# Attention and experts on one core: output products behind the value products, scores re-dealt over the units, the fourth gather ahead of a low half

## The chip, the cores and the metric

The kernel runs on one core of one Trainium2 chip. The metric is the device time of one execution in microseconds. Before the change: median 290.72 us of 3 runs (289.91 to 291.37).

## What is computed

The input x has 4 x 512 tokens of 512 channels. Per token it is normalized; then an attention with 8 heads of 8 channels over each batch of 512 tokens, and an expert layer with two experts of eight per token, are both applied to the normalized rows and added to x:

```python
xn  = layernorm(x)
qk  = (xn @ Wqk.T + bqk)  -> q, k of 8 heads, 8 channels each;   v = xn @ Wv.T + bv
att = softmax(q @ k.T, axis=-1) / sqrt(64)
a   = (att @ v) @ Wo.T + bo
y_e = relu(xn @ We[e] + be[e]);   top 2 of (xn @ Wgate + bgate)
out = x + a + mean over the two chosen experts of y_e
```

Everything is to be exact to fp32 closely, so products are made of a high and a low part of their operands.

## The kernel before

**Projection and routing** (lines 1235 to 1394). The 16 row tiles are normalized (ScalarE, row_mid), written to DRAM as xn_rows, transposed on TensorE and projected to q, k, v and gate logits. DVE then finds the two experts of each token; TensorE counts tokens per expert (counts, lines 1365 to 1375), DVE works out the place of each token in a list of 39 tiles of 128 rows, sorted by expert (lines 986 to 1022), and sets gather_i (the rows to gather) and expert_i (the expert of each tile; semaphore experts_known). The list is known a little before the gathers can deliver, and TensorE fills the time with matmuls that nothing reads ("unread").

**Expert tiles** (lines 1402 to 1430). For each of the 39 tiles POOL gathers 128 rows of xn_rows into one of six row_in buffers (gather, line 608; the first six at lines 615 to 620, with the low half of a weight chunk, low_half(7), ahead of the fourth). TensorE transposes tile n + 1 (turn_rows) and then multiplies tile n: 12 matmuls of 512 columns (line 1421), three for each of four channel blocks: t_hi by high weights, t_hi by low weights, t_lo by high weights. ScalarE makes t_hi from the transposed rows (774), DVE makes t_lo (1039). Behind tile n DVE adds the bias (1082), ScalarE does relu (779), POOL adds half of the output bias (637), SP stores the tile. The weights of experts 4 to 7 are split while the first tiles run: ScalarE the high part, DVE the low part (late_low, one chunk of 1024 columns at a time, line 1031), two before the loop, one in iteration 0 and one in each of iterations 1 to 5. DVE's iteration n is: t_lo of tile n, bias add of tile n - 1, then a late low half, then the maxima of tile n - 1.

**Scores and their ring.** Softmax needs each row's maximum ahead of the logits. So TensorE computes scores (queries by keys of one head, 32 rows of contraction, 512 columns, line 1283) into PSUM banks of a ring, DVE takes the maximum of each (line 1051), and the negated maxima are put into q_t as two more channels. Batches 0 and 1 have their scores behind the expert tiles: four behind each second tile from tile 5 on. In the tiles the ring has four banks. Batches 2 and 3 (64 scores) have theirs in the attention phase, where the ring has three banks.

**Attention units** (lines 1432 to 1451). A unit (b, u) is one batch, four heads and one block of 128 keys: 32 units. TensorE does for each: the first logit pair (two heads, line 1310), the unit's first half of scores, its jobs, the second logit pair, its second half of scores, and the value products of the unit before (line 1341, four heads side by side). ScalarE takes the exponential of each pair (line 818, 1024 columns). A pair waits until ScalarE has read the same pair's bank of the unit before; values wait for both exponentials of their unit.

Jobs (unit_jobs, line 257) are the further work that shares the ring: "k" and "q" (transposes of laid-out keys and queries, kept by ScalarE), "max" (transposes of the row maxima, kept by ScalarE), "o" (transposes of the value sums of the batch before; DVE divides them and splits them in lay_both, line 1104), "turn" (transposes back, waits for lay_both through o_laid, kept by ScalarE) and "out" (the output product, two matmuls at lines 1271 and 1272; DVE adds it to acc in result, line 1133, and SP stores it). In batches 1 to 3 unit 2 has "o", unit 3 "turn", units 4 to 7 "out" (in batch 3: two in unit 4, one in 5, one in 6). The list ring (lines 311 to 317) holds scores and jobs in TensorE's order; item n uses bank n mod 3 and waits until the item before it on that bank has been read. DVE serves its items in the same order: maxima of the first half, jobs, maxima of the second half. spread_scores (line 294) deals the 64 scores evenly over 48 half units from (0, 1) to (3, 0): one or two each, 2.67 per unit.

**Other queues.** POOL adds the experts' rows to acc by 32 indirect transfers during the attention. SP's queue, in order of code: loads of acc, move_max (eight small transfers that bring the maxima into q_t; the one for (2, 1) stands behind the first four stores), stores.

## Time and profile before

| | |
|---|---|
| median of 3 runs | 290.72 us (289.91 to 291.37) |
| profiled execution: its own time | 289.8 us |
| its span | 288.0 us |
| TensorE (PE) busy | 273.8 us (95%) |
| VectorE (DVE) busy | 211.6 us (73%) |
| ScalarE (ACT) busy | 162.1 us (56%) |
| GpSimd (POOL) busy | 193.3 us (67%) |
| projection and routing | 0 to about 58 us |
| expert tiles | about 60 to 198 us |
| attention units, with the last sums and stores | about 198 to 288 us |

"Busy" is the time in which an engine has an instruction under way. Matmuls are pipelined, so one of 512 columns is shown as 0.4 to 0.5 us while the next starts 0.23 us later: for TensorE, differences between starts say more than durations. "[0.69 <-DVE row_max L1051]" at the end of a timeline row means that the engine was idle 0.69 us before it and that this instruction of DVE released it.

### The profile page before, as it was taken

The page shows a single profiled execution, that of the slowest core. Times are in us where ns is not written, and L with a number is a line of the kernel's source. Part 1 is how long each engine was busy: PE and PEld are TensorE (multiplying, and loading weights), DVE is VectorE, ACT ScalarE, POOL GpSimd, SP SyncE. Part 2 cuts the span into 40 slices and gives each one's busy share as a digit, 9 for nine tenths or more (in the row PEclk, how much of TensorE's full clock was granted, in tenths as well). Part 3 has the DMA queues.
Part 4 walks back from the last instruction along what each step waited for, and adds up shares of the span by engine and source line. Part 5 has one row for each costly group of instructions (what it writes and reads, how often), then busy time and mean ns, then how long its engine had stood idle before and what let it go on. Part 6 is the DMA issues. An engine that isn't in the chain of part 4 may idle for free.

```text
span 288.0 us, 5481 instructions
## 1 busy us (share of the span) xinstructions
PE 273.8 (95%) x1685; PEld 180.2 (63%) x1685; DVE 211.6 (73%) x433; ACT 162.1 (56%) x241; POOL 193.3 (67%) x221
## 2 busy tenths in 40 slices
PE   6999998979999999999999999999999999999994
PEld 2699995567877777788777778774332333333342
DVE  2998898987877787767777776675678888784233
ACT  2669999256333333344333334436999878779861
POOL 3278997599866766898586866425788877887100
PEclk9799999799999999999999999999999999999999
DMA  7999899766544454435444445312599999999713
GB/s 213 388 400 397 287 278 404 268 225 201 178 164 148 146 146 149 147 110 184 148 149 147 150 146 150 110 73 75 190 221 262 262 253 236 198 209 183 158 67 146
DMA packets 28086, 57.35 MB, mean 199 GB/s; under 512 B 3287, under 2 KB 3608, under 8 KB 27804
## 3 DMA queue, kind: packets, MB, share of 16 engines
q1 hardware_dynamic: 19792, 37.59, 36.5%
q0 software_dynamic: 7728, 18.62, 30.0%
q10 hardware_dynamic: 540, 0.80, 0.8%
q8 instruction: 15, 0.25, 0.4%
q14 instruction: 11, 0.09, 0.1%
HBM read 38.29 MB, written 18.61 MB: 198 GB/s over the span
## 4 chain that ended last, share of the span: by engine, by line
PE 77%; DVE 8%; DMA 5%; issue 2%; POOL 2%; ACT 2%; SPq 1%; ACTq 0%; POOLq 0%
PE ps_l L1421 36%; PE ps_o L1341 7%; PE ps_l L1310 6%; PE ps_l L1399 6%; PE ps_l L1231 6%; PE ps_r L1283 3%; PE ps_l L1215 2%; PE ps_r L1259 2%; DMA w_split<-in_L_attn_Wv_w_dram 2%; DMA row_in<-xn_rows,gather_i 2%; DMA q_t<-max_rows 2%; PE ps_r L1271 2%; DVE row_max L1051 2%; ACT probs L818 1%; POOL row_in L612 1%
## 5 line engine op out<-in xcount | busy, mean ns | idle before, releaser
L1421 PE MATMUL ps_l<-w_split,t_hi 128*128 x312 | 100.1, 402 | 0.3 <-issue 0.3
L1051 DVE TENSOR_REDUCE row_max<-ps_r 128x1 f32<-128x512 f32 x112 | 73.0, 682 | 10.1 <-PE ps_r L1283 9.9
L637 POOL TENSOR_TENSOR row_mid<-row_mid,bias_o 128x512 f32<-128x512 f32 x39 | 51.4, 1319 | 35.5 <-ACT row_mid L779 35.4
L779 ACT ACTIVATE row_mid<-row_mid 128x512 f32<-128x512 f32 x39 | 24.7, 633 | 84.0 <-DVE row_mid L1082 84.0
L818 ACT ACTIVATE probs<-ps_l 128x1024 f32<-128x1024 f32 (+1 forms) x63 | 62.0, 1012 | 11.7 <-PE ps_l L1310 11.2
L1421 PEld LDWEIGHTS ps_l<-w_split,t_hi 128*128 128x128 f32 x312 | 55.8, 189 | 10.7 <-issue 0.8
L1421 PE MATMUL ps_l<-w_split,t_lo 128*128 x156 | 61.3, 393 | 0.0
L674 POOL DMA_INDIRECT acc<-expert_rows,slots_i x32 | 49.6, 1551 | 12.9 <-issue 7.2
L1082 DVE TENSOR_TENSOR row_mid<-ps_l,bias_e 128x512 f32<-128x512 f32 x39 | 27.0, 691 | 32.8 <-PE ps_l L1421 32.7
L612 POOL DMA_INDIRECT row_in<-xn_rows,gather_i x39 | 40.8, 1046 | 9.1 <-issue 2.9
L1421 PEld LDWEIGHTS ps_l<-w_split,t_lo 128*128 128x128 f32 x156 | 29.3, 188 | 6.6
L1283 PE MATMUL ps_r<-k_t,q_t 32*128 32x512 f32 x112 | 32.5, 489 | 0.2
L1310 PEld LDWEIGHTS ps_l<-q_t,k_t 32*128 32x128 f32 x124 | 11.3, 181 | 32.7 <-ACT probs L818 18.6
L1310 PE MATMUL ps_l<-q_t,k_t 32*128 32x512 f32 x124 | 29.7, 492 | 0.8 <-DMA q_t<-max_rows 0.4
L1039 DVE TENSOR_TENSOR t_lo<-ps_l,t_hi 128x512 fp32r<-128x512 f32 x39 | 26.9, 690 | 4.7 <-ACT t_hi L774 4.0
L1399 PE MATMUL ps_l<-ident,row_in 128*128 128x128 f32 x156 | 24.4, 279 | 1.6 <-DMA row_in<-xn_rows,gather_i 1.6
L774 ACT ACTIVATE t_hi<-ps_l 128x512 fp32r<-128x512 f32 x39 | 22.7, 582 | 3.8 <-PE ps_l L1399 3.8
L1399 PEld LDWEIGHTS ps_l<-ident,row_in 128*128 128x128 f32 x156 | 17.7, 141 | 8.8 <-issue 5.1
L1231 PE MATMUL ps_l<-wp_hi,t_hi 128*128 128x208 f32 x64 | 18.9, 295 | 1.0 <-DVE t_lo L919 0.4
L570 POOL TENSOR_TENSOR w_split<-w_split 128x1024 fp32r<-128x1024 f32 x8 | 19.0, 2395 | 0.6 <-ACT w_split L712 0.6
L1231 PE MATMUL ps_l<-wp_lo,t_hi 128*128 128x208 f32 x64 | 17.8, 278 | 0.0
L1231 PE MATMUL ps_l<-wp_hi,t_lo 128*128 128x208 f32 x64 | 17.7, 277 | 0.0
(218 smaller groups left out, 402.0 us busy)
## 6 DMA issues: line engine op xcount, KB each, us to landing
expert_rows<-row_mid SPq DMA_DIRECT2D x39, 256.0 KB, 2.0
xn_rows<-row_mid SPq DMA_DIRECT2D x16, 256.0 KB, 5.2
w_split<-in_L_ffn_W_e_dram SPq DMA_DIRECT2D x8, 512.0 KB, 5.6
w_split<-in_L_ffn_W_e_dram SPq DMA_DIRECT2D x4, 1024.0 KB, 11.0
acc<-in_L_attn_x_dram SPq DMA_DIRECT2D x16, 256.0 KB, 10.0
out_dram<-res SPq DMA_DIRECT2D x16, 256.0 KB, 3.7
row_in<-in_L_attn_x_dram SPq DMA_DIRECT2D x8, 256.0 KB, 5.9
w_split<-in_L_attn_x_dram SPq DMA_DIRECT2D x8, 256.0 KB, 7.1
```

The lines of the kernel that those rows point to most:

```text
L612: pool.indirect_dma_start(row_in[:, n % RI, :], None, xn_dram, bass.IndirectOffsetOnAxis(ap=gather_i[:, n:n + 1], axis=0)).then_inc(rows_i ...
L637: pool.tensor_tensor(row_mid[:, n % 4, :], row_mid[:, n % 4, :], bias_o[:], ALU.add).then_inc(y_done, 1)
L674: pool.indirect_dma_start(acc[:, i, :], None, y_dram, bass.IndirectOffsetOnAxis(ap=slots_i[:, r, i:i + 1], axis=0), compute_op=ALU.add).th ...
L818: act.activation(probs[:, n % 2, 2 * half:2 * half + 2, cs], logit_pair(half)[:, :, cs], ACT.Exp).then_inc(exp_done, 1)
L1039: dve.tensor_tensor(t_lo[:, n % 2, :], ps_t[:, n % 2, :], t_hi[:, n % 2, :].bitcast(F32), ALU.subtract).then_inc(rows_lo, 1)
L1051: dve.tensor_reduce(row_max[:, b % 2, h, i:i + 1], ring_bank(item), AX.X, ALU.max).then_inc(freed_by_dve, 1)
L1082: dve.tensor_tensor(row_mid[:, (n - 1) % 4, :], ps_y[:, (n - 1) % 2, :], bias_e[:, bass.ds(e, 1), :].rearrange("p a h -> p (a h)"), ALU.ad ...
L1231: mm = pe.matmul(ps_y[:, i % 2, 0:PW], a[:, i % 2, ks], w[:, c, :], start=(n == 0), stop=(n == 3 * KC - 1))
L1283: pe.matmul(ring_bank(item), q_t[b][rows, g, i * P:(i + 1) * P], k_t[b][rows, g, :], start=True, stop=True).then_inc(scores_ready, 1)
L1310: mm = pe.matmul(logit_pair(half)[:, k, :], k_t[b][rows, g, kt * P:(kt + 1) * P], q_t[b][rows, g, :], start=True, stop=True)
L1399: mm = pe.transpose(ps_t[:, n % 2, c * P:(c + 1) * P], row_in[:, n % RI, c * P:(c + 1) * P], ident[:])
L1421: mm = pe.matmul(ps_y[:, n % 2, :], a[:, n % 2, ks], rhs, start=(k == 0), stop=(k == 3 * KC - 1))
```

## The change

- In units whose jobs are all "o" or "out" (jobs_behind, but not (3, 6)), TensorE runs the jobs behind the value products, DVE serves them behind the maxima of the second half, and the ring lists them there. These are (1, 2), (1, 4) to (1, 7), (2, 2), (2, 4), (2, 6), (2, 7), (3, 4) and (3, 5). Units with a "turn", and (2, 5), which has a "max" too, keep their order.
- Scores are dealt by shares: units with an "o" or an "out" have 2, the others 3. It comes to two in ten units, three in twelve, four in (1, 3) and (3, 0).
- The four scores of tile 5 are put ahead of the first tile, between three and six unread matmuls that take the place of ten.
- POOL issues the fourth gather ahead of the low half.
- DVE's late low halves: none in iteration 0, one in each of iterations 1 to 6. They get a semaphore of their own, late_lo_made.
- The count of each expert gets P/2 - 0.5 from one more matmul (a new bf16 tile, rounding, with its semaphore; their declarations are left out below), and DVE takes the larger of that and P/2 + 0.5 where it added P/2 - 0.5, so an expert without tokens gets a tile too.

```diff
--- before.py
+++ after.py
@@ -53,6 +53,7 @@
 FIRST_UNIT_AT = NS - 2
 assert SCORES_AT[0] + H * QT // 2 <= SCORES_AT[1] and SCORES_AT[1] + H * QT // 2 <= FIRST_UNIT_AT
 FIRST_HALF, HALVES = 2, 48
+LIGHT, FULL = 2, 3
 BY_ROWS = [(b, g) for b in range(B - 1) for g in range(G)]
 
 
@@ -265,6 +269,10 @@
                     6: [("out", b - 1, 2)], 7: [("out", b - 1, 3)]}.get(u, [])
             return plan + (last if b >= 1 else [])
 
+        def jobs_behind(b, u):
+
+            return bool(unit_jobs(b, u)) and all(job[0] in ("o", "out") for job in unit_jobs(b, u)) and (b, u) != (B - 1, 2 * HG - 2)
+
         def tile_jobs(n):
 
             return {14: [("max", 0, 0)], 18: [("k", 1, 0), ("k", 1, 1)],
@@ -295,9 +303,17 @@
 
             halves = [[] for t in range(2 * 2 * HG * B)]
             left = [("score", b, g * HG + j, i) for b in range(2, B) for g in range(G) for i in range(QT) for j in range(HG)]
+            shares = [0]
+            for k in range(HALVES // 2):
+                b, u = divmod(FIRST_HALF // 2 + k, 2 * HG)
+                shares.append(shares[-1] + (LIGHT if any(job[0] in ("o", "out") for job in unit_jobs(b, u)) else FULL))
+
+            def due(k, part):
+                return (2 * H * QT * shares[k] + part * shares[-1]) // (2 * shares[-1])
+
             for k in range(HALVES):
                 t = FIRST_HALF + k
-                for n in range(2 * H * QT * k // HALVES, 2 * H * QT * (k + 1) // HALVES):
+                for n in range(due(k // 2, k % 2), due(k // 2 + 1, k % 2)):
                     taken = [item[2] % HG for item in halves[t]] + [2 * (t % 2), 2 * (t % 2) + 1]
                     item = [item for item in left if item[2] % HG not in taken][0]
                     left.remove(item)
@@ -314,7 +330,10 @@
         for b in range(B):
             for u in range(2 * HG):
                 t = 2 * (2 * HG * b + u)
-                ring += half_scores[t] + unit_jobs(b, u) + half_scores[t + 1]
+                if jobs_behind(b, u):
+                    ring += half_scores[t] + half_scores[t + 1] + unit_jobs(b, u)
+                else:
+                    ring += half_scores[t] + unit_jobs(b, u) + half_scores[t + 1]
         in_tiles = 4 + sum(len(tile_scores(n) + tile_jobs(n)) for n in range(NS))
         last_jobs = [job for u in range(HG, 2 * HG) for job in unit_jobs(B - 1, u)]
         in_bank = {item: n % (RING + 1) if n < in_tiles else (n - in_tiles) % RING for n, item in enumerate(ring)}
@@ -531,6 +550,7 @@
             pool.affine_select(out=ident[:], in_=ident[:], compare_op=ALU.not_equal, fill=1.0, base=0,
                                pattern=[[-1, P]], channel_multiplier=1).then_inc(consts_ready, 1)
             pool.memset(eps_t[:], EPS).then_inc(consts_ready, 1)
+            pool.memset(rounding[:], (P / 2 - 0.5) / P).then_inc(rounding_set, 1)
             link(pool.memset(ones[:], 1.0))
             pool.affine_select(out=before[:], in_=ones[:], compare_op=ALU.is_gt, fill=0.0, base=0,
                                pattern=[[1, P]], channel_multiplier=-1).then_inc(consts_ready, 1)
@@ -615,8 +635,9 @@
             for n in range(RI):
                 if n == 3:
 
+                    pool.wait_ge(experts_known, 1)
+                if n == 4:
                     low_half(NW - 1)
-                    pool.wait_ge(experts_known, 1)
                 gather(n)
 
             pool.wait_ge(half_bias, 1)
@@ -849,7 +870,7 @@
                     for half in range(2):
                         if 2 * n + half > 2:
                             exponentials(n, half)
-                        if half == 0:
+                        if half == jobs_behind(b, u):
                             for job in unit_jobs(b, u):
                                 if job[0] in KEPT:
                                     keep(*job)
@@ -983,7 +1004,7 @@
             dve.wait_ge(counted, 1)
             ps_c = ps_y[:, 0, 0:(NT + 1) * NE].rearrange("p (i e) -> p i e", e=NE)
 
-            link(dve.tensor_scalar(ecol[:, 1, :], ps_c[:, NT, :], P / 2 - 0.5, BY_128, ALU.add, ALU.add))
+            link(dve.tensor_scalar(ecol[:, 1, :], ps_c[:, NT, :], P / 2 + 0.5, BY_128, ALU.max, ALU.add))
 
             dve.wait_ge(ramp_ready, 4)
             link(dve.scalar_tensor_tensor(out=tri[:], in0=ecol[:, 1:2, :].to_broadcast([P, NE, NE]), scalar=-BY_128, in1=lower_ps,
@@ -1029,7 +1050,7 @@
                 dve.wait_ge(w_hi_made, c + 1)
                 cs = slice(2 * half, 2 * half + 2)
                 dve.tensor_tensor(w_split[:, e, 1, cs, :], w_split[:, e, 1, cs, :].bitcast(F32), w_split[:, e, 0, cs, :].bitcast(F32),
-                                  ALU.subtract).then_inc(w_lo_made, 1)
+                                  ALU.subtract).then_inc(late_lo_made, 1)
 
             dve.wait_ge(wo_split, 1)
             dve.tensor_tensor(by_columns(wo_lo), wo_ps, by_columns(wo_hi).bitcast(F32), ALU.subtract).then_inc(wo_split, 1)
@@ -1068,8 +1089,6 @@
             for n in range(NS + 1):
                 if n < NS:
                     rows_low(n)
-                if n == 0:
-                    late_low(NW + 2)
                 if n >= 1:
                     e = dve.value_load(expert_i[0:1, n - 1:n], min_val=0, max_val=NE - 1)
                     dve.wait_ge(y_made, n)
@@ -1083,8 +1102,8 @@
                                       ALU.add).then_inc(y_biased, 1)
                     if n == NS - 1:
                         lay_max(1, 1)
-                    if NW + 2 + n < 2 * NE:
-                        late_low(NW + 2 + n)
+                    if NW + 1 + n < 2 * NE:
+                        late_low(NW + 1 + n)
                     for item in tile_maxima(n - 1):
                         maximum(item)
                         if item == group_scores[item[1], item[2] // HG][-1] and n < NS - 2:
@@ -1157,7 +1176,7 @@
                             maximum(item)
                             if item == group_scores[item[1], item[2] // HG][-1]:
                                 lay_max(item[1], item[2] // HG)
-                        if half == 0:
+                        if half == jobs_behind(b, u):
                             serve(unit_jobs(b, u))
 
             def lay_half(piece):
@@ -1368,6 +1387,8 @@
             for i in range(last):
                 behind = NT - i
                 pe.matmul(counts[:, i + 1:NT + 1, :], ones[:], mask[:, i:i + 1, :].to_broadcast([P, behind, NE]), start=False, stop=False)
+            pe.wait_ge(rounding_set, 1)
+            pe.matmul(counts[:, NT, :], ones[:], rounding[:], start=False, stop=False)
             unread(2)
             pe.wait_ge(mask_ready, 3)
             pe.matmul(counts[:, last, :], before[:], mask_last[:, 0, :], start=False, stop=False)
@@ -1387,7 +1408,7 @@
             mm.then_inc(tokens_found, 1)
             for job in ring[2:4]:
                 fill(*job)
-            unread(10, D, ps_y[:, 0, :])
+            unread(3, D, ps_y[:, 0, :])
 
             def turn_rows(n):
                 pe.wait_ge(rows_in[n % RI], 16 * (n // RI + 1))
@@ -1399,6 +1420,9 @@
                     mm = pe.transpose(ps_t[:, n % 2, c * P:(c + 1) * P], row_in[:, n % RI, c * P:(c + 1) * P], ident[:])
                 mm.then_inc(rows_turned, 1)
 
+            for item in tile_scores(SCORES_AT[0]):
+                scores(item)
+            unread(6, D, ps_y[:, 0, :])
             pe.wait_ge(experts_known, 1)
             turn_rows(0)
             for n in range(NS):
@@ -1412,7 +1436,10 @@
                     pe.wait_ge(y_biased, n - 1)
                 if n < NE:
                     pe.wait_ge(w_hi_made, 2 * (n + 1))
-                    pe.wait_ge(w_lo_made, 2 * (n + 1))
+                    if n < LATE:
+                        pe.wait_ge(w_lo_made, 2 * (n + 1))
+                    else:
+                        pe.wait_ge(late_lo_made, 2 * (n + 1 - LATE))
                 k = 0
                 for c in range(KC):
                     ks = slice(c * P, (c + 1) * P)
@@ -1421,7 +1448,7 @@
                         mm = pe.matmul(ps_y[:, n % 2, :], a[:, n % 2, ks], rhs, start=(k == 0), stop=(k == 3 * KC - 1))
                         k += 1
                 mm.then_inc(y_made, 1)
-                for item in tile_scores(n):
+                for item in tile_scores(n) if n != SCORES_AT[0] else ():
                     scores(item)
                 for job in tile_jobs(n):
                     if job[0] == "first":
@@ -1441,7 +1468,7 @@
                         values(0, 0)
                     if n == LAST:
                         logits(b, u, 1)
-                    for job in unit_jobs(b, u):
+                    for job in unit_jobs(b, u) if not jobs_behind(b, u) else ():
                         fill(*job)
                     if n < LAST:
                         logits(b, u, 1)
@@ -1449,6 +1476,8 @@
                         scores(item)
                     if n >= 2:
                         values(*divmod(n - 1, 2 * HG))
+                    for job in unit_jobs(b, u) if jobs_behind(b, u) else ():
+                        fill(*job)
             values(B - 1, 2 * HG - 1)
             for kind, part in TAIL:
                 if kind == "o":
```

## Rows read from the trace of the kernel before

**Rows 1.** Waits of PE from 57 us on; us in total, times, longest us.

```profile
PE ps_l L1399 <- DMA row_in<-xn_rows,gather_i: 1.6, 3, 0.7
PE ps_r L1267 <- DVE row_max L1051: 1.1, 2, 0.7
PE ps_r L1249 <- DVE row_max L1051: 0.6, 1, 0.6
```

**Rows 2.** Busy time by stretch of units: us, PE, PEld, DVE, ACT, POOL, PEclk, DMA, GB/s.

```profile
200.10:218.16 18.06, 17.35 (x128) 6.30 (x124) 13.38 (x23) 17.03 (x23) 13.89 (x16) 1.00 0.80 209
219.98:225.61 5.63, 4.94 (x41) 1.84 (x37) 5.33 (x12) 4.92 (x6) 4.78 (x6) 1.00 1.11 263
225.61:236.31 10.70, 10.70 (x71) 3.75 (x67) 9.36 (x17) 8.40 (x9) 8.59 (x6) 1.00 1.11 256
236.31:246.65 10.34, 9.35 (x72) 3.19 (x68) 8.73 (x18) 8.76 (x11) 8.07 (x6) 1.00 1.12 232
246.65:258.13 11.48, 11.36 (x71) 4.15 (x72) 9.19 (x15) 8.66 (x9) 9.54 (x7) 1.00 1.04 202
258.13:262.23 4.10, 3.78 (x33) 1.14 (x29) 2.59 (x6) 3.56 (x5) 3.49 (x3) 1.00 1.06 217
```

**Rows 3.** Timeline, 59 to 67 us: POOL and PE; start us, us, engine line.

```profile
59.22 2.38 POOL L570 TENSOR_TENSOR w_split<-w_split 128x1024 fp32r<-128x1024 f32 x1
...
61.77 1.77 POOL L612 DMA_INDIRECT row_in<-xn_rows,gather_i  x1 [0.16 <-issue]
...
66.88 0.65 PE L1399 MATMUL ps_l<-ident,row_in 128*128 128x128 f32 x4 [0.29 <-DMA row_in<-xn_rows,gather_i]
```

**Rows 4.** Busy time of one microsecond before the tiles; PEclk is the third from the end.

```profile
52.00:53.00 1.00, 0.93 (x14) 0.58 (x15) 0.88 (x3) 0.00 (x0) 0.00 (x0) 0.51 1.08 438
```

**Rows 5.** Timeline of PE: first matmuls of tiles 5, 6 and 7.

```profile
76.89 0.71 PE L1421 MATMUL ps_l<-w_split,t_hi 128*128 x2
...
80.68 0.70 PE L1421 MATMUL ps_l<-w_split,t_hi 128*128 x2
...
83.88 0.71 PE L1421 MATMUL ps_l<-w_split,t_hi 128*128 x2
```

**Rows 6.** Timeline of DVE: last late low half, bias add of tile 5.

```profile
77.45 1.21 DVE L1031 TENSOR_TENSOR w_split<-w_split 128x1024 fp32r<-128x1024 f32 x1
...
80.05 0.69 DVE L1082 TENSOR_TENSOR row_mid<-ps_l,bias_e 128x512 f32<-128x512 f32 x1 [0.64 <-PE ps_l L1421]
```

**Rows 7.** Timeline of DVE: four maxima back to back, behind lay_both.

```profile
222.87 2.59 DVE L1051 TENSOR_REDUCE row_max<-ps_r 128x1 f32<-128x512 f32 x4
```

**Rows 8.** Timeline of PE in unit (1, 5): product, second pair, values; next unit.

```profile
228.78 0.50 PE L1271 MATMUL ps_r<-wo_hi,o_t 128*128 128x512 f32 x1
...
229.44 0.50 PE L1310 MATMUL ps_l<-q_t,k_t 32*128 32x512 f32 x2
...
229.87 1.05 PE L1341 MATMUL ps_o<-probs,v_second 128*18 128x512 f32 x8
230.85 0.50 PE L1310 MATMUL ps_l<-q_t,k_t 32*128 32x512 f32 x2
```

**Rows 9.** Timeline of PE in the last unit: both logit pairs, values.

```profile
276.10 0.70 PE L1310 MATMUL ps_l<-q_t,k_t 32*128 32x512 f32 x4
276.73 0.62 PE L1341 MATMUL ps_o<-probs,proj 128*9 128x256 f32 x8
```

**Rows 10.** Timeline of ACT: exponentials back to back, and of unit (1, 5).

```profile
218.79 3.77 ACT L818 ACTIVATE probs<-ps_l 128x1024 f32<-128x1024 f32 x4
...
228.88 2.12 ACT L818 ACTIVATE probs<-ps_l 128x1024 f32<-128x1024 f32 x2 [0.61 <-PE ps_l L1310]
```

**Rows 11.** Timeline: transposes of the sums, start of lay_both, the turn.

```profile
220.42 0.66 PE L1263 MATMUL ps_r<-ident,o_sum 128*128 128x128 f32 x4
...
221.17 0.35 DVE L1098 RECIPROCAL o_inv<-ps_r 128x32 f32<-128x32 f32 x1
...
223.61 0.66 PE L1267 MATMUL ps_r<-ident,o_tok 128*128 128x128 f32 x4 [0.69 <-DVE row_max L1051]
```

3 lines of the change are left out of this document (added).

## Prediction

> **What bounds the kernel now.** The page first: TensorE is busy for nearly all of the span and the other engines are not. But a full TensorE row does not mean that its order is free: where a matmul waits for a bank inside a group, the profile draws a longer busy stretch. So the waits come next, then the timeline round each place that the change touches. After the routing three waits stand out: 1.6 us for gathered rows, 1.1 us before the "turn" transposes and 0.6 us before the "max" ones, the last two for DVE's row maxima [rows 1]. Then I cut the attention phase at the first logit pairs of units [rows 2], since a unit's period is what this change is paid in: (1,4) to (1,7), each with one output product, take 10.70 us, 2.68 each.
>
> **Before the tiles.** POOL starts the low half (2.38 us) at 59.22 and issues gather 3 only at 61.77; its rows reach TensorE at 66.88, after 0.29 us of idleness [rows 3]. With gather 3 ahead, it goes out near 59.4, its rows land before 65 and tile 2 starts 0.3 earlier. The low half then ends near 63.4 and gather 4 goes out about when it does now; experts_known, now waited for first, is set long before. The low half is for tile 3, some seven microseconds later. **0.3 gained** (0 to 0.5).
>
> Three unreads, four scores and six unreads take the place of ten unreads. The four scores lie in four row groups, so they run together. The cover is TensorE's wait for the first gather, the longest of the three, 0.7 [rows 1]; without it the scores would cost 0.6. I take nothing (bound: 0.3 lost). TensorE's clock was at 1.2 GHz (0.51) in this stretch, where it had idled and then run small matmuls [rows 4].
>
> What the scores should bring in tile 5: that tile takes 3.79 us start to start with them, the next 3.20 without [rows 5], so 0.59. But the last late low half moves into DVE's iteration 6, where two maxima stand. From the tile's end DVE then does the bias add (0.6 to its next start), the low half (1.21) [rows 6] and two maxima (0.64 each) [rows 7] before t_lo of tile 7 (0.69): 80.05 + 0.61 + 1.22 + 1.28 + 0.69 = 83.85, where TensorE would want it at 83.88 - 0.59 = 83.29 [rows 5]. It waits 0.6, and the gain is gone. **Net 0** (0.6 gained to 0.2 lost). The other late low halves come a tile later into iterations without maxima. The rounding matmul runs while TensorE waits for mask_last, POOL's memset lies in its early slack, add and max are one DVE instruction either way, and two semaphores in place of one change no time of arrival: nothing. With the cover gone each would cost under 0.3.
>
> **Products behind the values.** Such a unit now runs: first pair and score (0.43 to the next start, like the second), product (0.66), second pair (0.43), values (0.98), 2.50 in all [rows 8]. Its three sisters share the other 8.20, 2.73 each; they have three scores: a score waits for the ring's bank. Behind the values, the two pairs touch each other. The last unit's two pairs take 0.63 without scores [rows 9]; with two scores I take 0.70. Period 0.70 + 0.98 + 0.67 = 2.35. ScalarE allows it: an exponential starts 0.54 after its pair (228.88; the pair 0.44 before the product of 228.78), and four back to back take 3.77, 0.94 each [rows 10], so the next unit's second pair may start some 0.54 + 0.94 + 0.94 + 0.14 for the last one's end = 2.56 after this unit's first. From there pair, values and product are 2.08 more: 4.64 for two units, 2.32 each. So 10.70 becomes 9.40: **1.3 gained** (0.3 to 2.0). The Trainium skill (TensorEngine Tiling (Array Packing), Key Properties) says that a change of tiling mode drains TensorE; three changes in place of four would by that save one drain, and the trace agrees: a lone pair 0.43, two together 0.63.
>
> (2,4) to (2,7) take 11.48 [rows 2]. Three go to 2.35. In (2,5), which keeps its order, the second pair's score waits now for the bank of ("max",3,0), freed by ScalarE behind an exponential; the new ring puts it on a bank that DVE frees sooner, and I take 2.9. Sum 9.95: **1.5 gained** (0.4 to 2.0). (3,4) and (3,5), three products in two units, by the same differences: **0.35 gained** (0 to 0.6).
>
> **Sums behind the values.** Here the move costs. The transposes of the sums start at 220.42, 0.44 into unit (1,2); lay_both begins 0.75 after and lasts 1.70 to DVE's next instruction; one maximum later the turn's bank is free, 223.61, 3.63 into a stretch of 5.63 [rows 2, 7, 11]. After: the second pair waits for ScalarE until 0.80, values at 1.23, sums at 2.2, lay_both 2.96 to 4.7, turn at 4.8, since it now waits for lay_both itself. Then the second pair (5.39), and DVE's maxima of (1,3)'s two first scores, queued behind lay_both: (1,3) has four scores, and the fourth uses the bank of the second, free at 6.04. Values 6.46, next unit 7.44. **1.8 lost** (0.6 to 2.1). In (2,2) and (2,3) the turn's unit has three scores, so that last wait is absent: about 6.85. Before them (2,0) gets a third score on the bank of its first; DVE has the result of ("out",0,3) and that maximum to do, so it goes at 1.45 and the unit takes 2.9, and (2,1) some 1.85. Together 11.6 against 10.34 [rows 2]: **1.2 lost** (0 to 1.6). SP issues store(3) ahead of move_max(2,1); its result comes later but before the maximum is kept, so the moves wait for nothing new.
>
> **More scores in the full units.** Of 24 units 14 now have three or four, 10 have two. (0,1), (0,4) and (0,7) gain one. ("max",1,1) in (0,2) waits 0.6 for DVE already [rows 1]; with one maximum more ahead of it (0.64), unit (0,3) starts 0.65 later. The other two lose 0.3 each, as their second score waits for a bank. ScalarE hides little of it: it is busy 17.03 of 18.06 there [rows 2]. **1.25 lost** (0 to 1.9). (3,0) gets a fourth score on its own first one's bank, behind a result: (3,0) and (3,1) take 4.55, now 4.10 [rows 2]: **0.45 lost** (0 to 1.0).
>
> **Sum.** -0.3 + 0 - 1.3 - 1.5 - 0.35 + 1.8 + 1.2 + 1.25 + 0.45 = +1.25. The profiled execution took 289.8 us (span 288.0), 0.9 under the median, so by it the changed kernel would take 291.0, and by the median 290.72 + 1.2 = **291.9**. A measurement of this kernel tells some 0.5%, 1.45 us, from no change; this is inside.
>
> **Rivals.** *The losses are absorbed* (faster). Each loss is a wait for a bank or for lay_both that I put on the path in full. If ScalarE's queue, nearly full before (1,2), sets the period there, the added scores and (2,0) lose nothing (1.25 + 0.45 + 0.8, the 0.8 for (2,0), = 2.5 less), and tile 5 may keep half of its 0.6. For: 17.03 of 18.06. Against: the 0.6 before "max" shows TensorE on the path. 1.25 - 2.5 - 0.3 = -1.55: 289.2.
>
> *The ring of three binds in the full units* (slower). A unit with three scores and a job takes four turns of three banks. If each of the ten or so such units up to (2,3) loses 0.17 beyond my terms, the sum is +2.95: 293.7. It decides once DVE no longer idles ahead of a unit's first maximum; it is busy 5.33 of 5.63 in the stretch from 219.98 [rows 2]. The Trainium skill (the same page, PSUM Bottleneck) warns that after fourfold tiling the copies out of PSUM may bind; the trace agrees for that stretch alone.
>
> *The clock falls in the turn's longer stall* (slower). TensorE would stand for some 1.5 us in (1,3). Should the clock go to 1.2 GHz as before the tiles [rows 4], four microseconds at half rate cost up to 2: 293.9. Against: with today's stall it stayed at 1.00 [rows 2]. The Trainium skill (TensorE: Matmul & The Clock Gate, What's actually happening) calls the throttled state the default that activity releases.
>
> That the change does not do what it says can hold for the scores in the gap alone, and is in the sum.
>
> **How the numbers follow.** Forecast 0.47, its own range 290.4 to 293.2; it lies close to the bound, so 0.35 of it counts as no change and 0.12 as slower. Absorbed 0.32 (0.25 faster, 0.07 no change). Ring 0.16, clock 0.05. Faster 0.25, same 0.42, slower 0.33. The range takes in the absorbed case and nearly the ring's, and so most of the bounds of the terms, which hardly fall all on one side: 288.9 to 293.6.
>
> **What would show it.** Right: turn 00 about 4.8 us behind the start of (1,2), with DVE's lay_both named; (1,4) to (1,7) in 9.4; tile 2 0.3 earlier; a new wait of 0.6 before tile 7; (2,0) near 2.9. Wrong: product units still at 2.5, or at 2.1; the turn at 3.6; (0,2) to (1,2) no longer than now; a granted clock below 1 after the tiles have begun.

## The result, and the profile after

The changed kernel took 294.64 us (median of 4 runs, 294.16 to 296.58) against 290.32 for the kernel before in the same comparison: ratio 1.0164, 95% interval 1.0101 to 1.0228. It is slower, by over three times the 1.25 us forecast, and above the range (288.9 to 293.6). The profiled execution took 294.16 us, span 292.4; before 289.8 and 288.0. Ratios here leave out executions that took over 1.5% more than the fastest of their kernel, so they can lie below the ratio of the medians.

The four largest waits of TensorE from 57 us on: engine, line and releaser; us in total, times, longest.

```profile
PE ps_r L1286 <- DVE o_tok L1133: 4.6, 2, 3.0
PE ps_l L1420 <- DMA row_in<-xn_rows,gather_i: 2.1, 2, 1.3
PE ps_l L1448 <- issue: 0.8, 2, 0.6
PE ps_r L1302 <- DVE row_max L1072: 0.8, 2, 0.6
```

L1286 is the turn (L1267 before), and its two waits have gone from 1.1 us for a row maximum [rows 1] to 4.6 for `o_tok`, the last operation of lay_both. That wait was forecast, though not 3.0 us of it in one piece.

The attention phase, cut at first logit pairs as in [rows 2]: (0,1) to (1,1), (1,2) and (1,3), (1,4) to (1,7), (2,0) and (2,1), (2,2) and (2,3), (2,4) to (2,7), (3,0) and (3,1), (3,2) to (3,6). Columns: us, PE, PEld, DVE, ACT, POOL, granted clock, DMA, GB/s.

```profile
197.78:221.00 23.22, 22.00 (x154) 7.64 (x153) 17.72 (x30) 19.83 (x26) 18.23 (x19) 1.00 0.81 206
221.00:228.42 7.42, 5.45 (x42) 2.01 (x38) 6.19 (x15) 5.12 (x6) 5.73 (x7) 1.00 1.10 261
228.42:237.69 9.27, 9.27 (x68) 3.14 (x64) 7.35 (x12) 7.58 (x8) 7.67 (x5) 1.00 1.12 237
237.69:242.45 4.76, 4.24 (x33) 1.25 (x32) 3.81 (x7) 4.03 (x7) 4.01 (x3) 1.00 1.11 278
242.45:252.32 9.87, 6.55 (x41) 2.30 (x38) 6.36 (x14) 5.23 (x6) 8.35 (x6) 0.83 1.02 171
252.32:262.26 9.94, 9.94 (x72) 3.55 (x68) 7.04 (x11) 8.20 (x9) 8.11 (x7) 1.00 1.04 192
262.26:267.08 4.82, 4.12 (x30) 1.21 (x29) 3.45 (x7) 3.82 (x6) 2.78 (x2) 1.00 1.05 229
267.08:280.52 13.44, 13.29 (x105) 5.67 (x101) 5.18 (x13) 11.73 (x14) 0.00 (x0) 1.00 0.34 90
```

Cut at the same places, the kernel before has 21.30, 5.64, 10.69, 4.18, 6.16, 11.48, 4.10 and 13.87 us. So the phase has grown by 5.32, and one stretch holds most of that: (2,2) and (2,3), 6.16 to 9.87, the only one with a clock below 1.00. (Unit (0,1) begins 0.9 earlier than before, and 0.8 of that is there already when the first tile's rows are transposed, at 57.34 against 58.14. It is not the change: the profiles below, which all have its first part, start there anywhere from 57.32 to 58.25. The span grows by 4.4.)

What happens in (1,3), TensorE first and then DVE:

```profile
223.21 0.66 PE L1282 MATMUL ps_r<-ident,o_sum 128*128 128x128 f32 x4
...
225.85 0.63 PE L1286 MATMUL ps_r<-ident,o_tok 128*128 128x128 f32 x4 [1.55 <-DVE o_tok L1133]
```

```profile
223.91 0.36 DVE L1117 RECIPROCAL o_inv<-ps_r 128x32 f32<-128x32 f32 x1 [0.84 <-PE ps_r L1282]
...
225.28 0.43 DVE L1133 TENSOR_TENSOR o_tok<-o_exact,o_tok 128x256 f32<-128x256 f32 x1
225.62 2.06 DVE L1072 TENSOR_REDUCE row_max<-ps_r 128x1 f32<-128x512 f32 x3
```

Sums at 2.2 into (1,2), lay_both from 2.9 to 4.6, turn at 4.85, three maxima queued behind. That is the forecast's sequence to 0.1 us. In (2,3) the same sequence looks like this:

```profile
244.72 0.66 PE L1282 MATMUL ps_r<-ident,o_sum 128*128 128x128 f32 x4
...
248.83 1.09 PE L1286 MATMUL ps_r<-ident,o_tok 128*128 128x128 f32 x4 [3.02 <-DVE o_tok L1133]
249.85 0.79 PE L1329 MATMUL ps_l<-q_t,k_t 32*128 32x512 f32 x2
...
250.58 1.81 PE L1360 MATMUL ps_o<-probs,proj 128*9 128x512 f32 x8
252.32 0.49 PE L1329 MATMUL ps_l<-q_t,k_t 32*128 32x512 f32 x2
```

```profile
246.60 0.36 DVE L1117 RECIPROCAL o_inv<-ps_r 128x32 f32<-128x32 f32 x1 [1.37 <-PE ps_r L1282]
```

And the single microseconds around it:

```profile
247.00:248.00 1.00, 0.00 (x0) 0.00 (x0) 0.93 (x3) 0.67 (x1) 0.90 (x1) 1.00 1.12 180
248.00:249.00 1.00, 0.17 (x1) 0.20 (x2) 0.96 (x3) 0.00 (x0) 0.69 (x2) 0.88 0.92 133
249.00:250.00 1.00, 1.00 (x7) 0.67 (x6) 0.89 (x2) 0.04 (x1) 1.00 (x1) 0.50 0.94 152
...
252.00:253.00 1.00, 1.00 (x13) 0.32 (x11) 0.10 (x1) 0.14 (x1) 0.69 (x2) 0.91 0.95 135
```

Read it in two parts. First, lay_both starts 1.88 us after the sums' transposes instead of 0.70, and the turn stands 6.4 into the pair of units instead of 4.85: 1.5 us that are lost before the clock column falls. Second, TensorE idles through 247 and most of 248, then comes back at 1.2 GHz until 252. Turn, pair and values take 1.02, 0.73 and 1.74 us start to start there, against 0.56, 0.43 and 0.97 in units at full clock: another 1.5 us. Together these are the 3.0 us by which the stretch misses its forecast of 6.85. (The whole fall lasts 3.4 us, from 248.76 to 252.17: it begins at the very end of the wait.)

A product unit (one with an "out" job) after the change, (1,5), values and product turned round against [rows 8]:

```profile
230.73 0.49 PE L1329 MATMUL ps_l<-q_t,k_t 32*128 32x512 f32 x2
...
231.42 1.05 PE L1360 MATMUL ps_o<-probs,v_second 128*18 128x512 f32 x8
232.41 0.50 PE L1290 MATMUL ps_r<-wo_hi,o_t 128*128 128x512 f32 x1
...
233.07 0.49 PE L1329 MATMUL ps_l<-q_t,k_t 32*128 32x512 f32 x2
```

Both pairs 0.69, values 0.99, product 0.66: 2.34, where 0.70, 0.98 and 0.67 were forecast.

In the expert tiles, POOL near 59 us, DVE and then TensorE near 81 us:

```profile
58.71 0.95 POOL L632 DMA_INDIRECT row_in<-xn_rows,gather_i  x1 [0.30 <-issue]
59.68 2.43 POOL L590 TENSOR_TENSOR w_split<-w_split 128x1024 fp32r<-128x1024 f32 x1
```

```profile
79.35 1.49 DVE L1052 TENSOR_TENSOR w_split<-w_split 128x1024 fp32r<-128x1024 f32 x1
80.76 1.28 DVE L1072 TENSOR_REDUCE row_max<-ps_r 128x1 f32<-128x512 f32 x2
81.96 0.68 DVE L1060 TENSOR_TENSOR t_lo<-ps_l,t_hi 128x512 fp32r<-128x512 f32 x1
```

```profile
81.65 0.60 PE L1420 MATMUL ps_l<-ident,row_in 128*128 128x128 f32 x4
82.84 0.72 PE L1448 MATMUL ps_l<-w_split,t_hi 128*128 x2 [0.59 <-issue]
```

Gather 3 now stands ahead of the low half, and tile 2 waits for no rows. The wait moved to tile 7 is there: DVE's low half, two maxima and t_lo are late by 0.6.

### The profile page after: what moved, and what is told of

Read it like the earlier page. It is cut to its first block, busy times and chain, and to the rows that moved or that the text cites. A ratio compares the mean times of both kernels' runs of the same rounds, so it can differ in the third digit from the quotient of the medians.

```text
span 292.4 us, 5482 instructions
## 1 busy us (share of the span) xinstructions
PE 272.5 (93%) x1685; PEld 179.3 (61%) x1685; DVE 211.6 (72%) x433; ACT 161.9 (55%) x241; POOL 195.9 (67%) x222
## 4 chain that ended last, share of the span: by engine, by line
PE 77%; DVE 14%; issue 3%; DMA 2%; ACT 2%; POOL 1%; SPq 0%; DVEq 0%; POOLq 0%; ACTq 0%
PE ps_l L1448 37%; PE ps_o L1360 9%; PE ps_l L1420 7%; PE ps_l L1329 5%; PE ps_l L1250 5%; PE ps_r L1302 3%; DVE row_max L1072 2%; PE ps_r L1278 2%; PE ps_r L1290 2%; DVE t_lo L940 1%; PE ps_l L1234 1%; DMA row_in<-in_L_attn_x_dram 1%; DMA row_in<-xn_rows,gather_i 1%; ACT probs L839 1%; PE ps_r L1282 1%
## 5 line engine op out<-in xcount | busy, mean ns | idle before, releaser
L658 POOL TENSOR_TENSOR row_mid<-row_mid,bias_o 128x512 f32<-128x512 f32 x39 | 50.6, 1297 | 32.9 <-ACT row_mid L800 32.3
L839 ACT ACTIVATE probs<-ps_l 128x1024 f32<-128x1024 f32 (+1 forms) x63 | 61.2, 1012 | 13.2 <-PE ps_l L1329 11.5
L632 POOL DMA_INDIRECT row_in<-xn_rows,gather_i x39 | 44.1, 1130 | 9.1 <-issue 3.6
L1302 PE MATMUL ps_r<-k_t,q_t 32*128 32x512 f32 x112 | 31.8, 486 | 1.3 <-DVE row_max L1072 0.8
L1329 PE MATMUL ps_l<-q_t,k_t 32*128 32x512 f32 x124 | 26.8, 488 | 0.6 <-issue 0.3
L1302 PEld LDWEIGHTS ps_r<-k_t,q_t 32*128 32x128 f32 x112 | 12.6, 182 | 8.8 <-issue 5.0
```

The lines of the kernel that those rows point to most:

```text
L632: pool.indirect_dma_start(row_in[:, n % RI, :], None, xn_dram, bass.IndirectOffsetOnAxis(ap=gather_i[:, n:n + 1], axis=0)).then_inc(rows_i ...
L658: pool.tensor_tensor(row_mid[:, n % 4, :], row_mid[:, n % 4, :], bias_o[:], ALU.add).then_inc(y_done, 1)
L839: act.activation(probs[:, n % 2, 2 * half:2 * half + 2, cs], logit_pair(half)[:, :, cs], ACT.Exp).then_inc(exp_done, 1)
L1302: pe.matmul(ring_bank(item), q_t[b][rows, g, i * P:(i + 1) * P], k_t[b][rows, g, :], start=True, stop=True).then_inc(scores_ready, 1)
L1329: mm = pe.matmul(logit_pair(half)[:, k, :], k_t[b][rows, g, kt * P:(kt + 1) * P], q_t[b][rows, g, :], start=True, stop=True)
```

## The experiments

The main theory: the sums behind the values make the turn wait for lay_both, the dealing of scores lengthens the full units, and on top the longer idleness lets TensorE's clock fall. The rivals: the clock is chance of an execution or chip and the price is that of the order alone; or one of the two parts carries all of it. The kernel before took 289.81 us (median of 22 runs), 290.02 (29) and 290.3 (23) in the three comparisons below. All experiments start from the changed kernel; e1 to e12 are the names that the quoted expectations use.

**e1.** **The changed kernel once more**, no edit.

> The changed kernel once more, to see which of its stalls come back. Theory (the turns wait for lay_both, and the longer of the two stalls lets the clock fall): the ratio is 1.012 to 1.020, the turn of (2,3) waits over 2 us again and TensorE's clock is at 0.5 in some four microseconds behind it. Rival (the 3.0 us stall and the clock fall are an accident of that one execution, and the kernel's steady loss is 1.8 in (1,3) plus the added scores): the turn of (2,3) waits some 1.6 us as that of (1,3) does, the clock stays at 1.00, and the span is some 3 us shorter than 292.4.

294.43 us (8 runs, 291.0 to 298.95), ratio 1.0094 (1.0055 to 1.0133). Every run comes with its mean granted clock, and among these eight the time goes with it: 291.0 at 0.988 and 291.15 at 0.994, but 298.77 at 0.951 and 298.95 at 0.954. Between kernels or series the mean is a poor guide, since it counts falls ahead of the tiles too: in the first four executions of this same program 0.988 goes with 294.16 and 294.76. The profile is of the 298.77 one. Its rows: (0,1) to (1,1), (1,2) and (1,3), (1,4) to (1,7), (2,2) and (2,3).

```profile
198.13:223.83 25.70, 24.25 (x155) 8.18 (x154) 18.00 (x30) 20.17 (x26) 19.41 (x20) 0.87 0.83 211
223.83:232.48 8.65, 6.39 (x43) 2.02 (x40) 6.73 (x15) 5.12 (x6) 7.36 (x7) 0.88 1.11 257
232.48:243.79 11.31, 11.31 (x69) 3.67 (x65) 7.00 (x11) 7.59 (x8) 9.48 (x7) 0.79 1.09 211
248.54:256.38 7.84, 6.00 (x41) 1.90 (x37) 5.78 (x14) 5.17 (x6) 6.62 (x5) 0.86 1.01 158
```

Three falls in one execution: 203 to 210, 230 to 237 and 254 to 258 us. Against the first profile of the same program the first costs 2.5 us (25.70 against 23.22), the second 3.3 (19.96 against 16.69, of which 0.3 is a longer wait). The turns waited 1.82 and 1.54 here, so the 3.0 of the first profile does not come each time, as the rival had it. The clock fell behind the turn of (2,3) again, as the theory had it. Falls come and go between executions of one program.

**e2.** **Sums and turn back in their old order**, products still behind the values, dealing as changed.

```diff
-return bool(unit_jobs(b, u)) and all(job[0] in ("o", "out") for job in unit_jobs(b, u)) and (b, u) != (B - 1, 2 * HG - 2)
+return bool(unit_jobs(b, u)) and all(job[0] == "out" for job in unit_jobs(b, u))
```

> The changed kernel with the sums of (1,2) and (2,2) back between the logit pairs; products stay behind the values, scores are dealt as in the change. Theory: nearly all of the loss is the two turns waiting for lay_both, so it takes 5 us less than the changed kernel, 289.5 to 290, a ratio of 0.995 to 1.000; (1,2) and (1,3) together take 5.6 to 6.2 in place of 7.4, (2,2) and (2,3) 6.0 to 6.4 in place of 9.9. Rival (DVE, late because of the four scores of (1,3) and the added scores before it, sets the turn whichever side the sums are on): the two pairs of units still take over 7 and 8, and the ratio stays above 1.010.

289.79 us (10 runs), ratio 1.002 (0.9991 to 1.0049). Rows as for the last kernel.

```profile
198.31:223.69 25.38, 24.18 (x154) 8.18 (x153) 17.73 (x30) 20.15 (x26) 19.81 (x21) 0.87 0.83 209
223.69:229.98 6.29, 5.41 (x43) 2.01 (x39) 6.06 (x15) 5.13 (x6) 5.52 (x6) 1.00 1.10 262
229.98:239.21 9.23, 9.23 (x70) 3.14 (x66) 7.35 (x12) 7.60 (x8) 7.49 (x6) 1.00 1.12 241
243.96:250.04 6.08, 5.18 (x43) 2.02 (x39) 5.71 (x14) 4.91 (x6) 5.17 (x4) 1.00 1.11 209
```

Moving the sums alone is worth the 4.6 us between this median and that of e1 (0.7% by the ratios). The two places where the order differs give 7.42 - 6.29 = 1.1 and 6.88 (from e5, below) - 6.08 = 0.8 of it at full clock. The other 2.7 us are not read off a stretch; what the profiles show beside the order is the falls behind the turns. The clock fell once here too, from 203 to 210, in (0,2) to (0,4), where the scores are dealt as changed. (The edit drops the exception of (3,6) as well, so its product stands behind its values here, in e6, e7, e11 and e12; the unit takes 2.96 against 2.94.)

**e3.** **The scores dealt evenly, as before; order as changed.**

```diff
-                for n in range(due(k // 2, k % 2), due(k // 2 + 1, k % 2)):
+                for n in range(2 * H * QT * k // HALVES, 2 * H * QT * (k + 1) // HALVES):
```

> The changed kernel with the scores dealt evenly over the 48 half units as before; sums and products stay behind the values. Theory (the dealing loses 1.9 before (1,2), 0.7 in (3,0) and 0.6 in (2,0), and gives back under 1 in the product units): some 2 us less than the changed kernel, a ratio of 1.005 to 1.010, with the turns' waits still there. Rival (the order alone makes the loss and the light units are what makes the product units fast): no less than the changed kernel, 1.015 or more, with product units at 2.5.

293.13 us (4 runs), ratio 1.0134 (1.0102 to 1.0165). The median is 1.3 us below that of e1, but the ratio is not lower, so the gain of 2 us that the theory had is not clear. (0,1) to (1,1) is back at 21.32, so the dealing made the +1.9 there. But (1,4) to (1,7) takes 10.62, nothing gained: (1,5), with two scores, takes 2.31, and of the three with three scores (1,4) takes 2.33 but (1,6) and (1,7) take 2.99 and 3.00, more than the 2.73 of three scores in the old order. The clock falls at 248 to 251, behind the turn of (2,3).

**e4.** **Both back; what is left is the change's first part** (gather, scores in the gap, late halves).

```diff
-return bool(unit_jobs(b, u)) and all(job[0] in ("o", "out") for job in unit_jobs(b, u)) and (b, u) != (B - 1, 2 * HG - 2)
+return False
...
-                for n in range(due(k // 2, k % 2), due(k // 2 + 1, k % 2)):
+                for n in range(2 * H * QT * k // HALVES, 2 * H * QT * (k + 1) // HALVES):
```

> Only what the change does ahead of the attention units: fourth gather first, scores in the gap, late low halves a tile later, the rounding matmul; order of jobs and dealing of scores are those of before. Theory: 0 to 0.4 us less than before, a ratio of 0.998 to 1.001; tile 2 starts without the wait for gathered rows and tile 7 waits some 0.6 for t_lo. Rival (the 0.59 of tile 5 is kept): a ratio of 0.996 to 0.997.

289.76 us (10 runs), ratio 0.9989 (0.9959 to 1.0019), as the theory had it. Its units take what they took before, within 0.05 in every stretch, and the clock does not fall from 57 to 285 us. So all of the loss is in the units, and the first part is worth nothing that can be measured.

**e5.** **The changed kernel with TensorE kept at work in the turns' stall.** Six matmuls of which nothing reads the result, behind the wait for the bank they write; the result of the kernel is the same.

```diff
+HELD = {(1, 3): 6, (2, 3): 6}
...
+                    if (b, u) in HELD:
+                        pe.wait_ge(exp_done, 2 * n - 2)
+                        unread(HELD[b, u], D, ps_y[:, 0, :])
```

> The changed kernel with six matmuls that nothing reads (512 columns, into the bank of the second logit pair, once its exponential is done) ahead of the turns of (1,3) and (2,3), inside the wait for lay_both. The waits for lay_both stay and TensorE is not idle in them. Theory (the changed kernel pays 1.8 and some 1.7 us for the waits themselves and, in most executions, 2 to 4 us more because TensorE's clock falls in or behind them): the clock is 1.00 from 225 to 285 in the profile, (1,3) still takes about 4.6 and (2,3) 4 to 5, the median is 291 to 292.5, a ratio of 1.005 to 1.009, and executions scatter less. A fall near 203, ahead of the first held turn, can still come. Rival (the clock falls for another reason than the idle turn, or costs nothing): the median stays at 294 and the clock still falls behind (1,3) or (2,3). Should the six cost more than the wait hides, (1,3) takes over 5.

TensorE and the microsecond behind the turn of (2,3):

```profile
245.48 1.47 PE L1377 MATMUL ps_l<-ones 128*128 128x512 bf16 x6
247.09 0.63 PE L1287 MATMUL ps_r<-ident,o_tok 128*128 128x128 f32 x4
247.65 0.50 PE L1330 MATMUL ps_l<-q_t,k_t 32*128 32x512 f32 x2
```

```profile
248.00:249.00 1.00, 1.00 (x11) 0.12 (x8) 0.83 (x2) 1.00 (x2) 0.69 (x2) 1.00 0.90 145
```

The filler delays the turn by nothing (it stands 4.91 into the pair of units, as in e1), and the clock stays: (2,2) and (2,3) take 6.88, against 9.87 and 7.84 in the two profiles of the changed kernel. But the median is 293.48 us (6 runs, 291.6 to 294.59), ratio 1.0125 (1.0089 to 1.0161): in its profile the clock fell at 263 to 266 instead, in (3,1), and (3,0) to (3,6) took 19.83 against 18.26. No wait of TensorE over 0.4 us stands in the ten microseconds ahead of that fall. So work in the gap of (2,3) went with a held clock there, in one profile, and holding two places doesn't hold the clock of the kernel. The expectation of a gain in the median was not met.

This profile also gives the price of order and dealing at full clock. Its units from (0,1) to (3,6) take 81.12 us; without the 1.6 of that fall (19.83 - 18.26) it is 79.5, against 77.4 in the kernel before: 2.1 us.

**e6.** **Products behind their values, scores dealt evenly, sums in their old place** (both edits shown above, that of the sums and that of the dealing).

> Products behind the values, scores dealt evenly as before, sums between the pairs, the edits ahead of the units as in the change: against e4_before_units it is the order of the products alone. Theory (with a third score the product unit waits for a bank in either order, 2.73 against 2.99; with two it takes 2.31 in place of 2.51, and (3,4) and (3,5) give 0.45): -0.1 to -0.6 us against e4, a ratio of 0.996 to 1.000. Rival (the order alone gives the 2.31 of the changed kernel in every product unit): 2.5 us less than e4, a ratio of 0.990.

289.09 us (12 runs), ratio 0.9978 (0.9951 to 1.0005), as the theory had it.

**e7.** **Scores dealt by hand**: two in a product unit, but never more than three in another, and none of the sums moved.

```diff
-FIRST_HALF, HALVES = 2, 48
-LIGHT, FULL = 2, 3
+FIRST_HALF, HALVES = 2, 50
+DEAL = ((1, 1), (2, 1), (1, 2), (2, 1), (2, 1), (1, 2), (1, 1),
...
-                for n in range(due(k // 2, k % 2), due(k // 2 + 1, k % 2)):
+                for n in range(DEAL[t // 2 - 1][t % 2]):
```

> The version that the readings point to: products behind the values, sums between the pairs, scores dealt over 50 half units: two in (0,1), (0,7), (2,0) and all units with a product, three in the others up to (3,1), so that no unit has four and (0,2) waits as before. Theory: the product units keep 2.31 (1.4 and 1.5 us gained), (3,4) and (3,5) 0.45; lost are some 0.5 in (0,4), 0.3 in (1,2), 0.2 in (2,3), 0.1 in (3,1). Sum -2.3: 287.5, a ratio of 0.990 to 0.994, and the clock stays at 1.00 from 60 to 285. Rival (the ring binds in the full units wherever the scores are put, so what is gained in the product units comes back there): a ratio of 0.998 to 1.003, with (2,0) to (2,4) and (3,0) to (3,2) longer than 10.34 and 4.10 by what the product units gain.

288.61 us (12 runs), ratio 0.9958 (0.9934 to 0.9982): 0.4% faster than the kernel before. It is short of the 287.5 expected; (3,2), which was not in the sum, takes 3.86 in place of 2.86.

**e8.** **The same dealing, with the products in the old order too** (the last edit, and jobs behind no unit's values).

> The dealing of e7 with all jobs between the logit pairs, as before the change: against e7 it is the order of the products with two scores each, against e4 the dealing alone. Theory: product units at 2.51 in place of 2.31, so 1.4 + 0.45 us more than e7, 289.4, and 0 to 0.7 less than e4. Rival (the fewer scores alone make the 2.31, since they take the bank waits away): the same time as e7.

289.48 us (12 runs), ratio 0.9995 (0.997 to 1.0021). The stretch (1,4) to (1,7) of the last three kernels in their order, even dealing with products behind, by hand with products behind, by hand with products between:

```profile
224.94:235.57 10.63, 10.36 (x71) 3.53 (x67) 9.04 (x16) 7.96 (x9) 8.25 (x6) 1.00 1.11 255
```

```profile
225.62:234.86 9.24, 9.24 (x69) 3.22 (x65) 7.30 (x13) 7.80 (x9) 7.71 (x6) 1.00 1.11 251
```

```profile
225.53:235.55 10.02, 10.02 (x68) 3.21 (x64) 8.21 (x14) 8.25 (x9) 8.01 (x6) 1.00 1.11 257
```

With the 10.69 of old order and even dealing (e4) all four combinations of two orders and two dealings are there. Order alone gives 0.06, dealing alone 0.67, both 1.45: under the even dealing (1,4), (1,6) and (1,7) have a third score, and in (1,6) and (1,7) it goes only 0.9 us into the unit (in (1,7) the trace names DVE's result, which frees its bank) and eats what the order saves. In (1,4) DVE had been idle for 0.72 us at its first maximum, and the third score costs nothing there.

**e9.** **Only the sums of (1,2) and (2,2) behind their values**, all else as in the kernel with both back.

```diff
+            return (b, u) in ((1, 2), (2, 2))
```

> Scores dealt evenly and products between the pairs, as before the change; only the sums of (1,2) and (2,2) stand behind their values (with the edits ahead of the units, as in e4_before_units). It is the price of that one move. Theory: the turns wait for lay_both, (1,2) and (1,3) take 6.8 and (2,2) and (2,3) 7.0 to 7.3 in place of 5.7 and 6.2, so 2 us more than e4 where the clock stays up and 3 to 4 where it falls: a median of 291.8 to 293.5, a ratio of 1.006 to 1.013, with the clock at 0.5 behind a turn in some executions. Rival (alone the move costs little, and it takes DVE's added maxima to make the turns late): less than 1 us over e4, under 1.003.

294.98 us (4 runs, 293.09 to 299.6), ratio 1.0135 (1.0035 to 1.0234). The windows of (1,3), of (2,3), and a microsecond of the latter:

```profile
222.63:226.94 4.31, 2.47 (x21) 0.92 (x21) 3.80 (x8) 2.32 (x3) 3.78 (x5) 1.00 1.10 261
244.60:249.80 5.20, 3.31 (x19) 0.92 (x18) 3.21 (x9) 2.54 (x3) 4.45 (x3) 0.82 1.07 180
248.00:249.00 1.00, 1.00 (x11) 0.10 (x8) 0.69 (x1) 1.00 (x2) 0.89 (x1) 0.50 1.08 172
```

Two groups of four transposes each, moved by one place, lose 1.35% by themselves, as much as the whole change does, and more than expected (the median was to be 291.8 to 293.5). The turns wait 1.84 and 1.89 us; the clock falls behind the second.

**e10.** **The changed dealing alone**, old order everywhere.

> The dealing of the change (two and three by shares, four in (1,3) and (3,0)) with all jobs between the pairs; edits ahead of the units as in the change. Theory: lost 1.9 before (1,2), 0.6 in (1,3), 0.9 in (2,0), 1 in (3,0), gained 0.2 in the product units that had three scores and 0.5 in (2,5), so 2.5 to 3 us over e4: 292 to 293, a ratio of 1.007 to 1.012, with a fall of the clock near 203 in some. Rival (fewer scores in the product units make up for it, as they do in e8): 290.5 or less, a ratio under 1.003.

Four runs, 290.97, 292.21, 296.21 and 296.76 us, at mean clocks of 0.994, 0.988, 0.965 and 0.97, too few and too far apart for a ratio. The two at high clock are 0.7 and 1.9 above the 290.3 of the kernel before, and the profile (of the 292.21) has 24.44 in (0,1) to (1,1) against 21.30, without a fall. So this part costs too, but how much beyond the stretches it lengthens is not settled.

**e11.** **By hand, with ("max", 3, 1) a unit later**, since (3,2) had grown to 3.86 us under the hand's dealing.

```diff
-(3, 2): [("max", 3, 1)]
+(3, 3): [("max", 3, 1)]
```

> The hand-dealt version e7 with the transposes of the last maxima in (3,3) in place of (3,2), where they wait for DVE's maxima of (3,0) and (3,1). Theory: (3,2) falls from 3.86 to about 2.5, (3,3) grows by 0.3 to 0.5: 0.9 us less than e7, 287.7, a ratio of 0.991 to 0.995. Rival (the turn of (3,3) takes the wait over): the same as e7, 0.995 to 0.997, with (3,3) at 3.6.

289.07 us (12 runs), ratio 0.9948 (0.991 to 0.9986). (3,2) to (3,6) falls from 14.45 to 13.51, and (2,2) grows, 7.04 for its pair of units against 6.35, so the gain expected in the median did not come. The ratio is that of the kernel dealt by hand within both intervals.

**e12.** **And with the late low halves as before**, so that tile 7 needs not wait.

```diff
+                if n == 0:
+                    late_low(NW + 2)
...
-                    if NW + 1 + n < 2 * NE:
-                        late_low(NW + 1 + n)
+                    if NW + 2 + n < 2 * NE:
+                        late_low(NW + 2 + n)
```

> e11 with DVE's late low halves back where they were before the change, one in iteration 0 and one in each of iterations 1 to 5, so that none shares an iteration with maxima. Theory (DVE's low half ahead of the two maxima delays t_lo of tile 7 and eats what tile 5 gains): the wait of 0.6 ahead of tile 7 is gone and the time is 0.6 to 0.8 less than e11's: a ratio of 0.989 to 0.993. Rival (another wait takes its place, or the early low half delays tile 1 instead): the same as e11, and tile 1 or 2 starts later by as much.

289.36 us (12 runs), ratio 0.996 (0.9922 to 0.9998), no gain over the last. Tile 7 starts 3.21 behind tile 6 without a wait, and tile 1 now waits instead, 0.89 (4.33 start to start against 3.18), as the rival had it. The DVE work of iteration 0 is that of the kernel before, where tile 1 waits for nothing, but here it takes longer: DVE's low half and POOL's, side by side:

```profile
60.05 3.82 DVE L1047 TENSOR_TENSOR w_split<-w_split 128x1024 fp32r<-128x1024 f32 x1
```

```profile
60.36 2.42 POOL L585 TENSOR_TENSOR w_split<-w_split 128x1024 fp32r<-128x1024 f32 x1
```

In the kernel before, POOL's began at 59.22 [rows 3] and DVE's, at 60.12, took 2.58; with no POOL low half beside it one takes 1.21 [rows 6]. So putting gather 3 ahead of POOL's low half and keeping DVE's in iteration 0 don't go together.

## Why the prediction was wrong

The terms as forecast, and as the profile of the changed kernel has them:

| term | forecast | measured |
|---|---|---|
| gather 3 ahead | -0.3 | -0.45 |
| scores out of tile 5, wait at tile 7 | 0 | -0.54 and +0.82 |
| scores before (1,2) | +1.25 | +1.92 |
| sums in (1,2), turn in (1,3) | +1.8 | +1.78 |
| products (1,4) to (1,7) | -1.3 | -1.42 |
| (2,0), (2,1) | +0.6 | +0.58 |
| sums in (2,2), turn in (2,3) | +0.7 | +3.71 |
| products (2,4) to (2,7) | -1.5 | -1.54 |
| (3,0), (3,1) | +0.45 | +0.72 |
| (3,4), (3,5) | -0.35 | -0.45 |

(The two tile terms come from the starts of the transposes that stand ahead of each tile's matmuls: tile 1 to 2 takes 3.19 against 3.65, tile 5 to 6 3.19 against 3.73, tile 7 to 8 4.54 against 3.72. The measured column adds up to +5.1 where the forecast had +1.25, 3.0 of the difference in one row.)

*Right:* the places of all ten, the signs of the nine that had one, and the size of six to within 0.2. The product units take 2.34 where 2.35 was worked out, (2,0) 2.94 and (2,1) 1.82 where 2.9 and 1.85 were, the turn stands at 4.85 where 4.8 was. The rule quoted there from the Trainium skill (TensorEngine Tiling (Array Packing), Key Properties), that a change of tiling mode drains TensorE, agrees with the rows: two pairs together take 0.69 to the values where each alone takes 0.43. That the drain is what they save is not shown, since matmuls of the two pairs also run side by side there. At full clock the whole of order and dealing costs 2.1 us in the units (e5), where the forecast had 1.55 (its sum without the 0.3 of gather 3). The two fastest executions of e1, 291.0 and 291.15, are 1.2 and 1.3 above the kernel before.

*Off in size:* (0,1) to (1,1) is 0.7 longer than summed, for (0,7) went from 2.44 to 3.24 and (0,4) from 2.43 to 2.94, where 0.3 was taken for each. The late low half took 1.49 us in place of the 1.21 of [rows 6], so tiles 5 and 7 together cost 0.3 where the net was to be 0.

*The step that failed:* the sum put the clock at nothing, and left it to the rival "The clock falls in the turn's longer stall", given 0.05 with the argument "with today's stall it stayed at 1.00 [rows 2]". Two things were wrong with it. The argument: the stall before was 0.7 [rows 1, 11], and the forecast itself lengthened it to some 1.5. And the form: it stood as an alternative to the sum, in (1,3) alone, where it adds to the sum at each place where TensorE newly stands. Its price was right: up to 2 us was put down, and the falls of 3.4 us cost 1.5 and 1.6, those of 6.8 us 2.5 and 3.3. An estimate from these numbers: with the losses as forecast and one such fall, the kernel comes out 2.8 to 4.6 us above the one before, and the medians are 4.3 and 4.6 above it. In the first profile itself one fall makes 1.5 of the 3.0 us by which (2,2) and (2,3) missed; the other 1.5, DVE's late start at the sums, was in no term either.

What speaks for it is, first, the set of profiles. At the turn of (2,3), the four with the sums behind and the gap empty have waits of 3.02, 1.54, 1.66 and 1.89 us (changed, changed again, even dealing, sums alone), and in all four the clock falls to 0.50 there, at the end of the wait in the first and 0.8 to 1.6 us behind it in the others. The one with the gap filled has none there, nor have the eight experiments and the kernel before whose sums stand in the old place, where the turn's wait is 0.41 to 1.02 (nine profiles in all). At the turn of (1,3) it is less sure: one fall behind waits of 1.55, 1.82, 1.54 and 1.84. So an idle stretch of 1.5 us or more was followed by a fall in five of eight cases. Second, the executions: of the 40 of kernels with the sums behind or the scores dealt as changed, 13 have a mean clock below 0.974; of the 74 of the kernel before and the 70 of the other six experiments, none has. But the idle stretch is not all of it: the falls at 203 us (e1, e2) and at 263 us (e5) have no wait of TensorE over 0.6 us in the ten microseconds ahead of them, and the changed dealing alone has two executions at 0.965 and 0.97. The forecast quoted the Trainium skill (TensorE: Matmul & The Clock Gate, What's actually happening), that activity releases the throttle; that did not make the fall unlikely. The same page (A second HAM failure mode: psum-queue depth-cycling) tells of a kernel whose short idle moments between groups of matmuls, while it cycles through PSUM banks, made the clock go to and fro between the two levels. The profiles here agree in kind; that section bore on the rival, and was not weighed.

*The rivals.* "The losses are absorbed" fell: (0,1) to (1,1) shows +1.9. "The ring of three binds" holds in part: the 0.7 there, and in e3 the 2.99 of product units with a third score.

*Left open:* in the first profile DVE and ScalarE got the results of the matmuls near 245 us some 1.2 us later than those of (1,2), before the clock fell. No other profile of that stretch has it, and its cause was not found. Also open is what decides whether a stall of a given length brings a fall, and what brought those at 203 us, in two of the five profiles with the changed dealing, and at 263 us.

## What to carry to other kernels

Price a new stall of TensorE, where it bounds the kernel, twice: its length, and the chance that the clock behind it halves (here 1.5 to 3.3 us a fall); add the second to the sum, and don't count the old, shorter stall as evidence that the clock holds. Two edits that look independent can need each other: in (1,4) to (1,7) the products' new order was worth 0.06 us with the scores dealt evenly and 0.78 with two in each unit, so test each edit with and without the other. When a chain (sums, lay_both, turn) has one unit to run in, moving its head back by 1.8 us moved the turn back by 1.2 and made the two units 1.8 longer; here the chain should have been left alone, and the kernel that does so and deals the scores by hand is 0.4% faster than the one before.

## What was not expected of the hardware

The granted clock fell to 1.2 GHz behind TensorE idleness of 1.54 us, for 3.4 us (other falls lasted 3.4 to 6.8 us), in a kernel whose TensorE is busy for 93% of the span. The same program took 291.15 us at a mean clock of 0.994 and 298.77 at 0.951, with three such falls after the routing. With six unread matmuls in the idle stretch the clock stayed up there, and nothing was delayed. DVE's last low half of 128x1024 elements takes 1.43 to 1.49 us instead of 1.21 in its new place, but 1.21 and 1.22 in e5 and e9, where it stands in the same place. The traces differ in what POOL does. Where an elementwise operation of POOL was under way when DVE's began, by 0.15 to 0.39 us of overlap, DVE's took 1.25 to 1.49, more with more overlap. Where POOL's began second, DVE's took 1.21 to 1.22 (1.28 and 1.29 at the first tiles) and POOL's 1.54 in place of 1.30. The 3.82 of e12 does not fit this order: POOL's low half began 0.3 us after it. No run was made to test it.
